# Feed-forward blocks 50 places behind their attention, and head sums as products of a high and a low part

## The reference

```python
x = x + _L0_attn_a_ref(_layernorm(x, axis=-1), ...)
x = x + _L0_ffn_ref(_layernorm(x, axis=-1), L0_ffn_Wg, L0_ffn_Wu, L0_ffn_Wd)
x = x + _L0_attn_b_ref(_layernorm(x, axis=-1), ...)
x = x + _L0_ffn_ref(_layernorm(x, axis=-1), L0_ffn_Wg, L0_ffn_Wu, L0_ffn_Wd)
```

```python
K = K * bt[..., None] + pk[:, :, None, :]
S = S * bt[..., None, None] + pk[:, :, None, :, None] * vt[:, :, None, None, :]
num = jnp.einsum('bhd,bhmdc->bhmc', pq, S)
den = jnp.einsum('bhd,bhmd->bhm', pq, K) + EPS
y = jnp.sum(num / den[..., None] * mt[..., None], axis=2)
```

## Time and profile before

| | us |
|---|---|
| median of 3 runs | 1718.75 (1716.77 to 1719.26) |
| the profiled execution | 1717.04 |
| its span | 1715.2 |
| PE busy | 1613.6 (94%) |
| DVE busy | 1075.4 (63%) |
| ACT busy | 1014.2 (59%) |
| POOL busy | 888.1 (52%) |
| first multiply of block tile 0 | at 112.3 |
| first multiply of block tile 3 (t = 5) | at 390.0, of tile 4 at 478.8 |
| last multiply of stage 1 | at 796.4 |

### The profile page before, as it was taken

How to read it: one execution, slowest core, us unless ns; L and a number is a source line. 1 busy time by engine, 2 the same in 40 slices (tenths; PEclk the granted TensorE clock), 3 DMA queues, 4 the chain that set the end, 5 groups by cost and what they waited for, 6 DMA issues and landing times. The chain is left out here.

```text
span 1715.2 us, 24775 instructions
## 1 busy us (share of the span) xinstructions
PE 1613.6 (94%) x7232; PEld 1247.1 (73%) x7232; DVE 1075.4 (63%) x1871; ACT 1014.2 (59%) x1872; POOL 888.1 (52%) x793
## 2 busy tenths in 40 slices
PE   3678999999999999999999999988999999999998
PEld 2356677878787878886666666656888888888887
DVE  5667778686869595557666666643454554554544
ACT  2237464646464646555887878875555555555554
POOL 3669764646454544362777777773333333333322
PEclk9789999999999999999999999998999999999999
DMA  3035543444443435541000000012555555555554
GB/s 106 1 111 184 189 138 132 143 142 148 148 148 128 148 130 184 205 177 57 1 1 1 2 0 1 1 38 99 187 193 203 201 187 190 197 193 205 194 187 135
DMA packets 72548, 215.88 MB, mean 126 GB/s; under 512 B 7387, under 2 KB 20832, under 8 KB 72416
## 3 DMA queue, kind: packets, MB, share of 16 engines
q1 hardware_dynamic: 72416, 214.35, 36.1%
HBM read 199.64 MB, written 14.68 MB: 125 GB/s over the span
## 5 line engine op out<-in xcount | busy, mean ns | idle before, releaser
L558 POOL TENSOR_TENSOR ARENA_R<-ARENA,ARENA_R 128x512 fp32r<-128x512 f32 x256 | 344.1, 1344 | 600.3 <-ACT ARENA_R L552 599.5
L582 DVE TENSOR_TENSOR ARENA<-ARENA,pair 128x512 f32<-128x512 f32 x512 | 349.1, 682 | 449.0 <-PE pair L345 410.4
L542 ACT ACTIVATE ARENA<-bank 128x512 f32<-128x512 f32 x512 | 306.1, 598 | 464.8 <-PE bank L345 463.0
L343 PE MATMUL pair<-ARENA_R 128*128 128x512 f32 x1064 | 417.1, 392 | 10.6 <-DVE ARENA L582 5.0
L345 PE MATMUL pair<-ARENA_R 128*128 128x512 f32 x1064 | 414.7, 390 | 0.0
L344 PE MATMUL pair<-ARENA_R 128*128 128x512 f32 x1064 | 414.2, 389 | 0.0
L552 ACT ACTIVATE ARENA_R<-ARENA 128x512 fp32r<-128x512 f32 x512 | 319.9, 625 | 36.1 <-DVE ARENA L582 33.6
L913 POOL TENSOR_TENSOR ARENA_R<-ARENA,ARENA_R 128x512 fp32r<-128x512 f32 x192 | 249.2, 1312 | 80.0 <-ACT ARENA L1120 76.6
L343 PE MATMUL bank<-ARENA_R 128*128 128x512 f32 x568 | 239.8, 422 | 23.0 <-DVE ARENA L1609 17.7
L343 PEld LDWEIGHTS pair<-ARENA_R 128*128 128x128 f32 x1064 | 200.7, 189 | 60.2 <-issue 7.3
L345 PEld LDWEIGHTS pair<-ARENA_R 128*128 128x128 f32 x1064 | 200.8, 189 | 42.4
(11 more groups left out here) (216 smaller groups left out, 2027.1 us busy)
## 6 DMA issues: line engine op xcount, KB each, us to landing
ARENA_R<-split_weights SPq DMA_DIRECT2D x360, 512.0 KB, 4.7
split_weights<-ARENA_R SPq DMA_DIRECT2D x24, 512.0 KB, 3.9
X<-in_L_attn_a_x_dram SPq DMA_DIRECT2D x8, 256.0 KB, 5.4
ARENA<-in_L_ffn_Wg_dram SPq DMA_DIRECT2D x8, 256.0 KB, 2.9
ARENA<-in_L_ffn_Wu_dram SPq DMA_DIRECT2D x8, 256.0 KB, 3.4
ARENA<-in_L_ffn_Wd_dram SPq DMA_DIRECT2D x8, 256.0 KB, 3.9
out_dram<-X SPq DMA_DIRECT2D x8, 256.0 KB, 4.2
CST<-in_tables_dram SPq DMA_DIRECT2D x1, 835.5 KB, 4.6
```

What stands on the lines that cost most here:

```text
L343: pe.matmul(dst, wh, xh, start=start, stop=False)
L542: act.activation(SG[:, c % 2, :], bank[c % 2], ACT.Silu).then_inc(F.sil, 1)
L558: eng.tensor_tensor(HL[:, G % FC, :], HF[:, G % FC, :], HH[:, G % FC, :].bitcast(F32), ALU.subtract).then_inc(lo_done(G)[0], 1)
L582: v.tensor_tensor(HF[:, c % FC, :], SG[:, c % 2, :], bank[2 + c % 2], ALU.mult).then_inc(F.mul, 1)
```

## The change

**The lag.** A generator `merged` takes the place of the two loops on every engine and pairs place c of step t with block cf of tile f, 50 places behind. So blocks begin at place 18 of step 1, and the last is at place 17 of step 9, where the loop ends. What belonged to the last step of the loop (`ramp`) is tied to the last block tile; the output of block tile 6 is added at fixed places.

**The sums.** ACT copies two products at a time to their high parts NUH (`product_hi`, places 18 and 20 for scale 0, 24 and 26 for scale 1), `product_lo` subtracts them for the low parts NUL (POOL at places 19 and 21 for scale 0, two each; DVE at 25 and 27 for scale 1), and PE sums both with fp32r matmuls against SUMR, a copy of the `sum_c`, at places 21, 23, 26 and 28. `weighted` of scale 1 goes from place 29 to 30, the sum of the scales from 30 to 31.

**Beside it.** Eight semaphores of attention B's projections become two counters. SP issues a weight set before the tables of stage 2, and these two sets later.

```diff
+LAG = 50
...
+        SUMR = sb("SUMR", [P, DA, P], F32R)
...
+        def product_lo(eng, t, m, p):
+
+            eng.wait_ge(A.nuh, 4 * t + 2 * m + p + 1)
+            if m == 0:
+                after(eng, A.num1, t)
+            else:
+                eng.wait_ge(A.num0, t + 1)
+            for i in range(2):
+                eng.tensor_tensor(NUL[:, p, i, :], S[:, m, 2 * p + i, :], NUH[:, p, i, :].bitcast(F32),
+                                  ALU.subtract).then_inc(A.nul, 1)
+
+        def merged():
+
+            for t in range(-1, NT + 2):
+                for c in range(CH):
+                    f, cf = divmod(CH * t + c - LAG, CH)
+                    if f < NT:
+                        yield t, c, f, cf
...
-                if x == NE * (NT - 2) + 5:
+                if x == NE * NT:
+                    sp.wait_ge(B.q2_ready, 2 * NSEQ)
+                if x == NE * NT + 1:
+                    sp.wait_ge(B.t_ready, UNITS * NSEQ)
+                for part in range(3):
+                    load_split(sp, x, part)
+                if x == NE * (NT - 2) + 7:
...
+            g.wait_ge(ld.tables_a, 16)
+            for c in range(DA):
+                g.tensor_copy(SUMR[:, c, :], cst(f"sum_{c}")).then_inc(pr.sumr, 1)
...
+                    if c in (19, 21):
+                        product_lo(g, t, 0, (c - 19) // 2)
-                    if c == 30:
+                    if c == 31:
...
+            def product_hi(t, m, p):
+
+                if m == 0:
+                    act.wait_ge(A.prod0, 3 * t + 2 + p)
+                    after(act, A.num1, t)
+                else:
+                    act.wait_ge(A.prod1, 5 * t + 3 + 2 * p)
+                    act.wait_ge(A.num0, t + 1)
+                act.activation(NUH[:, p, :, :], S[:, m, 2 * p:2 * p + 2, :], ACT.Copy).then_inc(A.nuh, 1)
...
+                    if c in (18, 20):
+                        product_hi(t, 0, (c - 18) // 2)
+                    if c in (24, 26):
+                        product_hi(t, 1, (c - 24) // 2)
...
-            def numerator(t, m, comps):
-
-                for c in comps:
-                    pe.wait_ge(*((A.prod0, 3 * t + 2 + c // 2) if m == 0 else (A.prod1, 5 * t + 2 + c)))
-                    x = pe.matmul(bank[(7, 6)[m]], cst(f"sum_{c}"), S[:, m, c, :], start=(c == 0), stop=(c == DA - 1))
-                if DA - 1 in comps:
+            def numerator(t, m, p):
+
+                pe.wait_ge(A.nul, 8 * t + 4 * m + 2 * p + 2)
+                for i in range(2):
+                    for part in (NUH, NUL):
+                        x = pe.matmul(bank[(7, 6)[m]], SUMR[:, 2 * p + i, :], part[:, p, i, :],
+                                      start=(p + i == 0 and part is NUH), stop=(p + i == 2 and part is NUL))
+                if p:
                     x.then_inc((A.num0, A.num1)[m], 1)
...
-                    if c == 20:
+                    if c == 21:
                         pe.wait_ge(a_used["v3"], t + 1)
-                        numerator(t, 0, (0, 1))
+                        numerator(t, 0, 0)
                     if c == 22:
-                        numerator(t, 0, (2, 3))
                         pe.wait_ge(a_used["v2"], t + 1)
                         denominators(t)
-                    if c == 24:
+                    if c == 23:
+                        numerator(t, 0, 1)
+                    if c == 26:
                         pe.wait_ge(n_a.lo, min(t + 2, NT))
                         after(pe, n_f.lo, t)
-                        numerator(t, 1, (0, 1))
-                    if c == 25:
-                        numerator(t, 1, (2, 3))
-                    if c == 26:
+                        numerator(t, 1, 0)
                         weights(t, 0)
+                    if c == 28:
+                        numerator(t, 1, 1)
                     if c == 27:
                         weights(t, 1)
...
+                    if c == 25:
+                        product_lo(v, t, 1, 0)
+                    if c == 27:
+                        product_lo(v, t, 1, 1)
                     if c == 28:
                         weighted(t, 0)
-                    if c == 29:
+                    if c == 30:
                         weighted(t, 1)
...
-            for t in range(-1, NT + 2):
-                for c in range(CH):
-                    f = t - 2
-                    if is_tile(f):
-                        ffn_dve(v, f, c)
-                    attn(t, c)
-                    if t == NT + 1:
-                        ramp(c)
+            for t, c, f, cf in merged():
+                if is_tile(f):
+                    ffn_dve(v, f, cf)
+                attn(t, c)
+                if f == NT - 1:
+                    ramp(cf)
```

More of the change, by code:

```diff
@@ L286, in program @@
         XAL = take(TOK, dt=F32R)
+        NUH = take(2, 2, TOK, dt=F32R)
+        NUL = take(2, 2, TOK, dt=F32R)
         at[F32R] = 0
@@ L708, in _ @@
                     sp.dma_start(BB[0:2, C:], row(b_bv).broadcast_to([2, DB])).then_inc(ld.bb, 16)
-                if x == NE * NT:
-                    sp.wait_ge(B.q2_ready, 2 * NSEQ)
-                if x == NE * NT + 1:
-                    sp.wait_ge(B.t_ready, UNITS * NSEQ)
-                for part in range(3):
-                    load_split(sp, x, part)
                 if x >= NE * (NT + 1) and x % NE == 6:
@@ L856, in rotated @@
                 name = "qk"[i]
[L857 to L858 removed]
+                after(g, *projected(b_used, nxt, name + "s"))
                 after(g, B.hi, 2 * nxt.n)
@@ L1064, in _ @@
             act.wait_ge(pr.bmix, 2)
[L1065 to L1076 removed]
+            for t, c, f, cf in merged():
+                if is_tile(f):
+                    if is_tile(f - 1) and cf == 3:
+                        take_down(act, f - 1)
+                    ffn_act(act, f, cf)
+                elif f == -1 and cf >= CH - FC and part_at(f, cf):
+                    hi_part(act, *part_at(f, cf))
+                attn(t, c)
+                if f == NT - 1:
+                    ramp(cf)
             hidden_hi(act, NT * CH - 1)
@@ L1230, in attn @@
                         project(t, "qs", bank[7])
-                if is_tile(f - 1) and c == 6:
+                if (t, c) == (NT, 24):
+                    pe.wait_ge(n_f.lo, NT)
+                    back(pe, NT - 2)
+                if 0 <= f - 1 < NT - 2 and c == 6:
                     if is_tile(t):
@@ L1355, in _ @@
             pe.wait_ge(pr.selr, 1)
+            pe.wait_ge(pr.sumr, DA)
             pe.wait_ge(pr.ba, 2)
-            for t in range(-1, NT + 2):
-                for c in range(CH):
-                    f = t - 2
-                    if is_tile(f):
-                        ffn_pe(pe, f, c)
-                    attn(t, c)
-                    if t == NT + 1:
-                        ramp(c)
+            for t, c, f, cf in merged():
+                if is_tile(f):
+                    ffn_pe(pe, f, cf)
+                attn(t, c)
+                if f == NT - 1:
+                    ramp(cf)
             down(pe, NT * CH - 3)
@@ L1649, in attn @@
                     a_stats(v, nxt)
-                if is_tile(f - 1) and c == 7:
+                if (t, c) == (NT, 25):
+                    residual(v, NT - 2)
+                if 0 <= f - 1 < NT - 2 and c == 7:
                     residual(v, f - 1)
```

61 lines of the change are left out of this document (23 added, 38 removed).

## The result

| | before | after |
|---|---|---|
| median, us | 1719.01 (1716.77 to 1719.66, 4 runs) | 1766.38 (1764.1 to 1767.41, 4 runs) |
| span of the profiled execution | 1715.2 | 1762.3 |
| last multiply of stage 1 | 796.4 | 842.1 |

The change makes the kernel slower: ratio 1.0275, 95% interval 1.0259 to 1.0291. The forecast was 1740 us with a range up to 1758: the direction was right, the loss twice the size forecast. Nearly all of it is in stage 1 (842.1 - 796.4 = 45.7 us of the 47.1 by which the span grew).

The account below looks back on a forecast made before the run. DVE and PE were both taken as full in places 9 to 25, PE alone elsewhere; tile 0 +4.7, lag -9.9 and seven stretches of 4.0 (+28) gave +22.8 on 1717.0, so 1740 us, range 1710 to 1758.

Parts of the forecast that it names:

- tile 0: Attention alone: nine instead of five POOL instructions end about 4.8 us later; +4 to +6, taken as +4.7 us.
- tile 1, places 18 to 31 (37.4 + 6 + 4 - 21.5): Joint places at 37.4 us, 6 for POOL's weight splits, 4 for the new sums, replace 21.5 us of attention alone.
- end, 14 places without attention: With the shorter lag, 14 block places without attention, 2.04 us each, go at the end: 28.6 us.
- what was to show it: Tiles near 93 us, PE waits at places 26 (2 to 4 us) and 21 (1 to 3, by POOL), sums 0.23 us apart.
- PE paces the whole tile: Rival: DVE is full only at PE's feeding rate, so each tile shortens by 3.2 us; 1682 us; 0.20 with a milder form.
- the walk: One steady tile followed from place 18's multiply (441.4): place 25's low parts done at 467.5, place 27's multiply at 471.0.
- the upper value: Cost of a steady tile with DVE's new subtractions at place 25 blocked by POOL: +4.8 us.
- I take +4.0: Cost taken for a steady tile's places 18 to 31, between +2.3 and +4.8 us, nearer the upper.
- then 0.9 us of sums, 1.0 of weight rows and refill and 1.4 of block: PE's work after its wait at place 26, putting the multiply of place 27 at 471.0, where it was at 467.1.
- ACT ... costs nothing by itself: ACT's four new 128x1024 copies a tile, 1.2 us each, 5 us in all beside 49.9 of 88.8, add no time.
- That excess of 3.2 us leaves tile 2: POOL's weight splits, which made tile 2's places 18 to 31 take 40.6 us, move to tile 1 with the lag.
- POOL sets the pace: Rival: every new POOL subtraction delays DVE by its full 1.28 us, 5.1 a tile; tile +7.4, 1767 us; chance 0.08.

Follow-up runs that it names:

- e3: The changed kernel with ACT's copy of the down product (L591) moved one place earlier, from block place 3 to the end of block place 2: 1765.5 us.
- e7: e3 with 14 matmuls on constants that nobody reads, put on PE ahead of the first sums of scale 1 at place 26: 1754.29 us.
- e5: The changed kernel without any low parts, the sums being of high parts alone (their matmuls on low parts go too): 1704.15 us.
- e9: The changed kernel without the low parts of scale 0, POOL's four; DVE's four stay: 1743.76 us.
- e10: The changed kernel without the low parts of scale 1, DVE's four; POOL's four stay: 1731.12 us.
- e6: The changed kernel with both the edit of e3 and the edit of e4: 1743.46 us.
- e4: The changed kernel with the first sums of scale 1 one place later on PE (27 for 26), behind a block and the first weight rows: 1738.78 us.
- e1: The lag of 50 alone, with the old fp32 sums at places 20 to 25: 1712.21 us, ratio 0.9962 against the kernel before.

## Why the prediction was right in sign and wrong in size

Its terms against the trace (places 18 to 31 from multiply to multiply):

| term | predicted | measured |
|---|---|---|
| tile 0 | +4.7 | +9.6 |
| tile 1, places 0 to 17 | 0 | +2.2 |
| tile 1, places 18 to 31 (37.4 + 6 + 4 - 21.5) | +25.9 | 49.6 - 21.5 = +28.1 |
| tile 2, places 0 to 17 | 0 | -1.5 |
| tile 2, places 18 to 31 (4 - 3.2) | +0.8 | 43.9 - 40.6 = +3.3 |
| tiles 3 to 7, places 18 to 31 | 5 x 4.0 | 219.7 - 187.2 = +32.5 |
| end, 14 places without attention | -28.6 | -28.6 |
| sum | +22.8 | +45.6 |

So the bottleneck and the sign were right, and the step that failed is the price of the added work. The sum priced a joint tile at +4.0, on PE's full pace behind the waits that it forecast and with nothing for ACT's copies; tiles 3 to 7 cost 6.5 us each. It also took tile 0 at +4.7 (9.6) and let 3.2 us leave tile 2 that stayed. The paragraphs below take these one by one.

Of what was to show it: steady tiles near 93 us are 94.6 and 96.4; the wait of place 26 is there, and that of place 21 too, but released by ACT and not by POOL (with the copy out of the way, e3 and e7 do show one of 2.1 us by POOL); the sums start 0.23 us apart where the clock is up; the first multiply of a block, forecast at 95 to 99 us, comes at 102.6.

**Right: what bounds the stage.** DVE's row with POOL's holds on it is the ceiling of places 17 to 25. e5 shows it from one side, e9 and e10 part by part. PE's saving of 3.2 us a tile bought nothing while the low parts were there (rival "PE paces the whole tile" is out). The reason given against that rival, that nothing removes a hold by POOL, is not right: in e5 ACT's new copies shift POOL's instructions, and DVE's row is 2.1 us shorter than before.

**Right in sum, in part by luck: the walk.** It put the end of the low parts of place 25 at 26.1 us behind the multiply of place 18 (467.5 - 441.4) and the multiply of place 27 at 29.6. In e7, where PE waits 0.5 us for the copy of the down product and has its full clock behind place 26, these are 26.0 and 29.6 (426.29 - 396.68). The four matmuls of place 28 add the 0.9 reckoned for them. That is the upper value, 4.8 us. But inside it two errors cancel. The walk had the multiply of place 25 "as now", 21.0 us behind that of place 18; in e7 it comes at 21.9, since two more scans are held. From there it gave 5.1 us to the end of the low parts; e7 takes 4.1, since these aren't held:

```profile
418.58 0.63 DVE L608 TENSOR_TENSOR ARENA<-ARENA,pair 128x512 f32<-128x512 f32 x1
...
420.04 1.52 DVE L1750 SCALAR_TENSOR_TENSOR ARENA<-ARENA 128x256 f32<-128x256 f32 x1
421.48 1.28 DVE L365 TENSOR_TENSOR ARENA_R<-ARENA,ARENA_R 128x512 fp32r<-128x512 f32 x2
```

And in the change itself the multiply of place 26 comes at 26.9 to 27.1 us in tiles 3 to 7, one more than in e7 (see below).

**Wrong: "I take +4.0".** The upper value held, for the reason that the text itself gave: POOL is busier, so more is blocked. From the multiply of place 18 to that of place 26, e7 has 3.5 us more of DVE work than the kernel before: 1.2 are its own two low parts, 2.3 are longer scans and weights beside POOL (the weights took 0.42 us before). POOL is held likewise, its low parts for 1.86 us in the mean of a steady tile instead of 1.28:

```profile
L365 POOL TENSOR_TENSOR ARENA_R<-ARENA,ARENA_R 128x512 fp32r<-128x512 f32 x4 | 7.4, 1864 | 0.0
```

Taking 4.0 for 4.8 us in each of five tiles is 4 of the 23 us missed.

**Wrong: no price for the wait itself.** The step "then 0.9 us of sums, 1.0 of weight rows and refill and 1.4 of block" took PE's pace from rows at clock 1.00 and applied it right behind a forecast wait of 2 to 4 us. In e3 that piece, from multiply 26 to 27, takes 6.4 us in the tile shown; in e7 3.6 us. In the change tiles 3 to 7 are 43.9 us in the mean, 1.7 more than this tile of e7; for five tiles that is 8.5 us, the larger part of what the steady tiles missed. Some 3.5 of them lie between the multiplies of places 26 and 27, nearly all in tiles 4 and 6, which work there at half clock (5.3 us; the other three take 3.7). The other 5.0 lie before the multiply of place 26 and come of the wait at place 21, which is the next point. The forecast named the waits and took the pace behind them for granted.

**Wrong: "ACT ... costs nothing by itself".** ACT had time, but its list has an order. The copy that waits for DVE holds up L591 and PE at place 21 for 3.8 us, and PE works at half clock behind it. With L591 moved (e3) the multiply of place 26 comes at 25.8 to 26.0 us in tiles 3 to 7, not at 26.9 to 27.1: that is the 1.0 us a tile. It isn't won by that move alone. e3 loses it again behind place 26 at half clock (5.3 us or more in four tiles) and is 0.9 us better than the change in all; in e6 PE sets the pace from place 26 on, and the tile is as long as in e4.

**Wrong: tile 0.** POOL's five products with the new low parts end 4.8 us later, at 59.7 instead of 54.9, as reckoned. What follows up to the output projection was counted at nothing more, and takes 11.4 us instead of 6.6. The windows of the two kernels for it, the change first:

```profile
59.70:71.10 11.40, 6.91 (x17) 4.54 (x17) 4.05 (x7) 2.25 (x3) 1.26 (x1) 0.70 0.01 1
```

```profile
54.90:61.50 6.60, 3.12 (x10) 1.74 (x10) 1.65 (x3) 1.19 (x2) 1.26 (x1) 1.00 0.01 2
```

The split puts copy, subtraction and sums in a row behind the last product (L996 at 59.72, L365 to 62.4), and the clock is 0.70 where it was 1.00, since PE waits 4.1 us for them. The rest is lag: tile 1 starts slower (+2.2) because block tile 0's weight splits now fall there (PE waits 1.9 and 0.4 us for their low parts before its first block), and e1 shows the same (32.2 us from the output projection to place 18, against 29.3).

**Wrong: "That excess of 3.2 us leaves tile 2".** Without POOL's new subtractions the prediction's terms for the lag are -12.7 - 3.2 + 3.2 = -12.7 us; e1's stage 1 is 6.8 us shorter. The excess does come up in tile 1 (44.0 us, 3.4 over the 40.6), but tile 2 keeps 40.2 of its 40.6 us in e1. In the change this is most of what tile 2 missed (+3.3 where +0.8 was reckoned).

**The rival "POOL sets the pace"** gave 1767 us, the measured time, and is still not the mechanism: the number came out by luck. It asked for 7.4 us a tile by longer blocking, 5.1 of it for POOL's four subtractions. Leaving these out (e9) shortens places 18 to 31 of tiles 3 to 7 by 3.1 us in the mean; without the 3.8 us wait and with the clock up behind place 26 the stretch costs 4.8 (e7); and in the change DVE is idle for 2.3 us in places 22 and 23, where that rival has it blocked. The Trainium skill, "SBUF — State Buffer", section "Who interferes with whom", says that the two exclude each other for a whole instruction. Its blunt reading stood for that rival; the trace agrees with the rule, not with that reading: scans of 1.21 us take 2.3 in e7 and none takes longer, as with turns in the earlier trace rows.

## What to carry to other kernels

Before an operation is split to relieve one engine, ask which engine ends the wait in that stretch: here PE was relieved by 3.2 us a tile, and DVE, already full, got four subtractions of its own and is held by four more on POOL. Ask also what a new wait in one engine's list holds up behind it (ACT's copy at place 20 held an old one, and PE with it). When a forecast has TensorE wait some microseconds, price the work behind the wait at half clock too, and try first to put a block or weight rows ahead of the waiting instruction (e4: 28 us). And test the parts of a double change apart: the lag alone is 1712.21 us, the better kernel.
